# Threshold sums moved among ScalarE's waits, and the work between two attention groups reordered, in a fused four-layer graph network kernel

## The reference

```python
Xf = Xa = X = h
Z = 0
for n in range(2):
    q = Xa @ W1.T @ W2.T
    k = Xa @ W3.T
    probs = softmax(q @ k.T)                      # 2048 x 2048
    # keep the largest probabilities of a row until their sum reaches 0.9
    A = probs * mask;  A = A / A.sum(-1)
    Xf = rownormed(adj + I) @ Xf
    Xa = A @ Xa
    Z = Z + Xf @ U1[n].T + Xa @ U2[n].T
x = x + layernorm(X + Z) * ln_g + ln_b
```

## Time and profile before

| | |
|---|---|
| median of three executions | 1072.57 us (1072.10 to 1072.85) |
| the profiled execution's own time | 1073.61 us |
| its span, first to last instruction | 1071.8 us |
| TensorE busy (products) | 838.4 us, 78% |
| VectorE busy | 779.4 us, 73% |
| ScalarE busy | 509.2 us, 48% |
| GpSimd busy | 70.5 us, 7% |
| TensorE's mean granted clock | 0.894 of full speed |

### The profile page before, as it was taken

The page is one execution under the profiler, slowest core; times in us unless marked ns, Lnnn a source line. Parts: engine busy times, 40 slices in busy tenths (PEclk is TensorE's granted clock), DMA queues, the critical chain, the costliest instruction groups (busy, mean ns, idle before and its releaser), DMA issues.

```text
span 1071.8 us, 12286 instructions
## 1 busy us (share of the span) xinstructions
PE 838.4 (78%) x3886; PEld 563.7 (53%) x3886; DVE 779.4 (73%) x2363; ACT 509.2 (48%) x979; POOL 70.5 (7%) x68
## 2 busy tenths in 40 slices
PE   4879958887887843839778978868289899996795
PEld 4844325555655633737356557547258475553342
DVE  5978679888998998961797889789799502326715
ACT  4877235357367376314452664764765332023212
POOL 0020110000000000000000000010000200002201
PEclk9999987888988985969799789979689999998798
DMA  9949203334004000000044220220152546500001
GB/s 335 354 173 430 104 29 129 130 106 158 1 1 158 1 1 1 1 2 1 1 157 149 87 79 1 94 119 1 49 209 78 230 161 245 226 1 0 1 0 39
DMA packets 20221, 108.25 MB, mean 101 GB/s; under 512 B 1824, under 2 KB 8752, under 8 KB 9776
## 3 DMA queue, kind: packets, MB, share of 16 engines
q1 hardware_dynamic: 18752, 106.77, 26.7%
q10 hardware_dynamic: 1392, 0.61, 0.2%
HBM read 88.23 MB, written 19.14 MB: 100 GB/s over the span
## 4 chain that ended last, share of the span: by engine, by line
PE 47%; DVE 29%; ACT 11%; issue 9%; POOL 2%; DMA 1%; DVEq 1%; POOLq 0%; SPq 0%; ACTq 0%
DVE AT L1525 9%; PE PS L808 9%; PE PS L743 7%; PE PS L676 5%; PE PS L880 5%; PE PS L546 4%; DVE mxv L1664 4%; DVE nd L1528 3%; PE PS L1063 3%; PE PS L1039 3%; DVE AT L2111 2%; PE PS L1069 2%; ACT BC L1252 2%; ACT AT L1252 2%; ACT AT L1085 1%
## 5 line engine op out<-in xcount | busy, mean ns | idle before, releaser
L1085 ACT ACTIVATE AT<-PS 128x512 f32<-128x512 f32 (+2 forms) x240 | 118.2, 562 | 127.1 <-PE PS L546 107.8
L743 PE MATMUL PS<-K,ST 128*128 128x512 f32 x224 | 129.4, 731 | 15.7 <-ACT EA L1220 8.1
L546 PE MATMUL PS<-ident,AT 128*128 128x128 f32 x544 | 84.1, 289 | 42.5 <-DVE AT L1525 18.0
L1525 DVE SCALAR_TENSOR_TENSOR AT<-EA,se 128x2048 uint8<-128x2048 f32 (+1 forms) x46 | 107.6, 2345 | 1.6 <-DVE se L1518 0.3
L1525 DVE SCALAR_TENSOR_TENSOR AT<-AT 128x2048 uint8<-128x2048 f32 (+2 forms) x48 | 96.1, 2002 | 1.8 <-PE PS L546 0.8
L1664 DVE TENSOR_REDUCE mxv<-PS 128x1 f32<-128x2048 f32 x32 | 73.3, 2289 | 30.4 <-PE PS L743 24.7
L546 PEld LDWEIGHTS PS<-ident,AT 128*128 128x128 f32 x544 | 67.5, 150 | 50.9 <-DVE AT L1525 18.9
L743 PEld LDWEIGHTS PS<-K,ST 128*128 128x128 f32 x224 | 50.6, 238 | 78.1 <-issue 78.0
L2111 DVE MAX8 AT<-AT 128x8 f32<-128x256 f32 x256 | 87.6, 411 | 0.7
L808 PE MATMUL PS<-hr,AT 128*128 128x128 f32 x512 | 69.2, 284 | 8.5 <-ACT AT L1085 7.7
L808 PE MATMUL PS<-AT 128*128 128x128 f32 x512 | 67.4, 279 | 10.2 <-ACT AT L1085 9.7
(11 more groups left out here) (297 smaller groups left out, 1471.1 us busy)
## 6 DMA issues: line engine op xcount, KB each, us to landing
AT<-keep_at SPq DMA_DIRECT2D x32, 1024.0 KB, 5.1
EA<-in_adj SPq DMA_DIRECT2D x20, 1024.0 KB, 6.8
keep_at<-AT SPq DMA_DIRECT2D x8, 2048.0 KB, 24.9
AT<-keep_at SPq DMA_DIRECT2D x8, 2048.0 KB, 12.2
AT<-in_adj SPq DMA_DIRECT2D x12, 1024.0 KB, 5.7
EA<-keep_degrees SPq DMA_DIRECT2D x1, 1024.0 KB, 6.4
keep_x<-K SPq DMA_DIRECT2D x4, 256.0 KB, 8.6
out<-EA SPq DMA_DIRECT2D x4, 256.0 KB, 2.3
```

Source lines behind the costliest of these rows:

```text
L546: return pe.transpose(dst, src, ident[0:p, 0:p])
L743: mm = pe.matmul(bank(half(gi, k) + n), ST[1][:, k * P:(k + 1) * P], wide_keys[:, n * BK:(n + 1) * BK], start=True, stop=True)
L1085: return act.activation(dst, src, ACT.Copy)
L1525: return dve.scalar_tensor_tensor(out=o, in0=x0, scalar=s, in1=x1, op0=op0, op1=op1, **k)
```

## The change

It moves instructions and adds no computation; no operand and no transfer is changed.

1. **TensorE, first round of a step.** A unit's product can be cut in halves. The logits of tile 2 go ahead of the rows of unit 1, and those of tile 3 between the halves of unit 2.
2. **ScalarE, first round.** The first-threshold sums of tiles 0 and 1 (four passes) no longer stand behind the queries: the first goes between the copy and the rows of the fourth unit, the second ahead of the queries, the third between the two query copies, the fourth behind them.
3. **ScalarE, second and third round** (the third only in step 0): one pass behind the last attended tile's fourth copy, one ahead of the queries (where there are any).
4. **ScalarE, every attended group's last tile:** `guess` goes ahead of the copy of the previous tile's result, where it stood behind it.
5. **VectorE, the six groups that have a successor in their step:** the last tile's mass goes ahead of the checks of `doubtful`, and these interleave with the sums.
6. **Step 1, third and fourth round:** the second norm and scaling of block 0 move ahead of the first-threshold sums; the norm of block 1 moves from the start of the fourth round to the third; its turning and summing on TensorE move one tile up.

```diff
 # TensorE
-            def unit_sums(u):
+            def unit_freed(u):
+
                 if u == UNITS:
                     pe.wait_ge(un_row, UNITS)
                 if u > 0:
                     pe.wait_ge(un_st, u)
                     pe.wait_ge(un_row, min(u, UNITS))
+
+            def unit_part(u, h):
+
+                p, c = u // UNITS, u % UNITS
                 left = hr if p == 0 else Xf
-                for j in range(NT):
-                    if j % HALF == 0:
-                        pe.wait_ge(slab_in[j // HALF], 16 * (u + 1))
+                pe.wait_ge(slab_in[h], 16 * (u + 1))
+                for j in range(h * HALF, (h + 1) * HALF):
...
-            def unit(step, g, u, early=False):
+            def unit_begun(step, g, u, early=False):
...
-                unit_sums(u)
+                unit_freed(u)
+                unit_part(u, 0)
+
+            def unit(step, g, u, early=False):
+
+                unit_begun(step, g, u, early)
+                unit_part(u, 1)
                 unit_rows(u)
...
-                if normed is not None and k - normed in (1, 2):
-                    rows_turned(normed, k - normed - 1)
+                if normed is not None and k in (1, 2):
+                    rows_turned(normed, k - 1)
...
-                    if normed == 1:
-                        pe.wait_ge(exT_ok, G * gi + k + 1)
-                        rows_summed(normed, 1)
...
+                            at = units_by(NB * step) + k
                             if k > 0:
                                 logits(step, 1, k)
-                            if k < UNITS_IN[NB * step]:
-                                unit(step, 0, units_by(NB * step) + k, True)
+                            if k == 2:
+                                unit_rows(at - 1)
+                            if k == 3:
+                                unit_part(at - 1, 1)
+                                unit_rows(at - 1)
+                            if k == 1 or k == 2:
+                                unit_begun(step, 0, at, True)
+                            if k == 1:
+                                unit_part(at, 1)
+                            if k == 0 or k == 3:
+                                unit(step, 0, at, True)
...
 # ScalarE
-            def queries(step, g):
+            def queries(step, g, between=None):
...
                 copy(ST[0][0:DA, :], bank(7)[0:DA, :]).then_inc(t1_out, 1)
+                if between:
+                    between()
                 act.wait_ge(q_mm, gi + 1)
...
+            def one_below(step, g, m, k, f):
+
...
+                act.activation(act_junk[f], E[:, k, :], ACT.Relu if f == 0 else ACT.Sign, scale=-1.0,
+                               bias=th[:, k:k + 1], accum_out=below[:, f, k:k + 1]).then_inc(sum_ok, 1)
...
                     copy(stg[b % 2], bank(4 + b % 2)).then_inc(e_copied, 1)
+                    if b == 1 and between:
+                        between()
                     if b == 1 and k > 0:
                         result_out(k - 1)
-                    if b == 1 and between:
-                        between()
                     if b == 2 and inside:
                         inside()
+                if copied:
+                    copied()
...
-                    if normed == 0:
-                        first_scaled(0)
-                    elif normed == 1:
-                        first_norm(1)
+                    if normed is not None:
+                        first_scaled(normed)
                     for k in range(G):
                         if g > 0:
-                            attend(step, g - 1, k, (lambda: guess(step, g + 1)) if more and k == G - 1 else None, normed,
-                                   inside=(lambda: exponential(step, g + 1, 1)) if more and k == 0 else None)
-                            if normed == 1 and k == 0:
-                                first_scaled(1)
+                            ends = more and k == G - 1
+                            attend(step, g - 1, k, (lambda: guess(step, g + 1)) if ends else None, normed,
+                                   inside=(lambda: exponential(step, g + 1, 1)) if more and k == 0 else None,
+                                   copied=(lambda: one_below(step, g + 1, 0, 0, 0)) if ends and normed is None else None)
+                            if ends and normed is None:
+                                one_below(step, g + 1, 0, 0, 1)
...
-                        if g == 0:
-                            if k == G - 1:
-                                guess(step, 1)
+                        if g == 0 and k != 2:
                             unit_next()
+                        if g == 0 and k == G - 1:
+                            guess(step, 1)
+                            unit_sums(u)
+                            one_below(step, 1, 0, 0, 0)
+                            unit_rows(u)
+                            u += 1
+                            one_below(step, 1, 0, 0, 1)
                     if g < NB - 2:
-                        queries(step, g + 2)
+                        queries(step, g + 2, (lambda: one_below(step, 1, 0, 1, 0)) if g == 0 else None)
+                    if g == 0:
+                        one_below(step, 1, 0, 1, 1)
                     if more:
-                        sums_below(step, g + 1, 0, (0, 1, 2))
-                        unit_next()
-                        if step == 1 and g == 1:
-                            first_norm(0)
                         if normed == 0:
                             second_norm(0)
-                            sums_below(step, g + 1, 1, (0,))
+                            sums_below(step, g + 1, 0, (0,))
                             second_scaled(0)
-                        sums_below(step, g + 1, 1, (1,) if normed == 0 else (0, 1))
+                            sums_below(step, g + 1, 0, (1, 2))
+                        else:
+                            sums_below(step, g + 1, 0, (2,) if g == 0 else (1, 2))
+                        unit_next()
+                        if step == 1 and g > 0:
+                            first_norm(g - 1)
+                        sums_below(step, g + 1, 1, (0, 1))
                         unit_next()
                         sums_below(step, g + 1, 1, (2,))
...
 # VectorE
+            def doubtful_with_sums(nq, n):
+
+                mass_above(EA if n % 2 == 0 else EB, n, G - 1)
+                v.wait(1)
+                v.put(tt(s_(3), s_(3), s_(4), ALU.max))
...
+                dve.wait_ge(sum_ok, sums_by(n, 0) + 2 * (G - 1))
+                v.put(stt(pa, below[:, 1, :], float(N), ALU.add, nq.th, ALU.mult))
...
+                crossing_checked(q)
                 if left > 1:
                     logit_mean(gi + 2)
-                crossing_checked(q)
-                doubtful()
-                if left > 0:
-                    last_tile(nq, gi + 1)
-                    surplus_below(nq, gi + 1, 0)
-                    last_surplus(nq)
+                if left == 0:
+                    doubtful()
+                else:
+                    doubtful_with_sums(nq, gi + 1)
```

59 lines of the change are left out of this document (37 added, 22 removed).

## The result

| | before | after |
|---|---|---|
| median | 1072.71 us (1072.10 to 1073.60, 4 runs) | 1086.65 us (1086.12 to 1087.79, 4 runs) |
| ratio, 95% interval | | 1.0131 (1.0113 to 1.0148) |
| span of the profiled execution | 1071.8 us | 1086.0 us (the slowest of its four) |

The account below looks back on a forecast made before the run. No engine bounds it throughout; a chain changing engines does, without slack from ScalarE's second query copy. Terms 3.0 + 2.6 + 0 + 0.8 + 2.5 - 6.2 = +2.7 us gave 1075.3 us against the median, range 1067.5 to 1080.0.

Parts of the forecast that it names:

- (d): Guess ahead of the result's copy: TensorE's projection starts 1.1 us later, offset by a 1.1 gain in step 0's third round.
- First rounds, TensorE's order: First rounds' earlier logits: VectorE 4.6 us earlier at its cut, fourth unit ready at 225.7, nothing gained.
- First rounds, passes: ScalarE's passes among its first-round waits: second query copy +2.6 us; total +3.0 in step 0, +0.8 in step 1.
- (e): Second rounds, ScalarE's pass behind the last attended tile's fourth copy: +0.6 us.
- (f): Second rounds, ScalarE's pass ahead of the queries: +0.8 us with the issue.
- Checks: VectorE's interleaved checks in step 0's third round: gain 1.1 us, for a round total of 0.
- Tail: Step 1 from the third round on, norms reordered: -6.2 us (-7.8 to -3.6), GpSimd's last root slipping ahead of VectorE's masks.
- boundary gives nothing away: Rival, chance 0.21: next logits don't hang on the second query copy, four boundary terms fall to 0; -6.5, 1066.1 us.
- passes hide better: Rival, chance 0.17: first query product at half clock in other rounds too, (b) and (f) cost nothing; 1072.3 us.
- the tail doesn't pay: Rival, chance 0.20: GpSimd's root starts behind VectorE's first mask, -3.6 to -4 instead of -6.2; 1077.7 us, up to 1080.
- five terms ahead of the tail: Step 0's first, second, third rounds +3.0, +2.6, 0; step 1's first and second +0.8, +2.5 us.

Follow-up runs that it names:

- e7: Kernel before with only ScalarE's four first-round passes moved among its waits: 1076.53 us, ratio 1.0046.
- e13: Changed kernel with VectorE's old checks restored and the mean of the logits ahead of the exact cut: 1087.59 us, ratio 1.0148 to the kernel before.
- e4: Kernel before with only VectorE's interleaved checks, the mean of the logits behind the exact cut: 1071.44 us, ratio 1.0001.
- e11: Kernel before with step 1's reordered norms and VectorE's interleaved checks, the mean behind the exact cut: 1070.83 us, ratio 0.9990.
- e14: Changed kernel without TensorE's new first-round order and the four first-round passes: 1084.97 us, ratio 1.0129 to the kernel before.
- e15: Same instructions as e11, kernel before with reordered norms and interleaved checks, run for a second profile: 1071.73 us, ratio 0.9992.
- e9: Kernel before with only ScalarE's early passes of the second rounds and step 0's third round: 1077.72 us, ratio 1.0040.
- e12: Kernel before with both first-round parts, TensorE's new order and ScalarE's four passes: 1080.64 us, ratio 1.0071.
- e3: Kernel before with only the reordered norms in step 1's third and fourth round: 1065.59 us, ratio 0.9935.
- e10: Same as e3, only the reordered norms in the kernel before, measured again: 1067.39 us, ratio 0.9946.
- e18: Same as e3, only the reordered norms in the kernel before, a third comparison: 1067.78 us, ratio 0.9954.
- e5: Changed kernel with TensorE's projection put behind the next blocks turned and multiplied: 1079.29 us, ratio 1.0055 to the kernel before.
- e2: Kernel before with only the guess moved ahead of the result's copy: 1081.60 us, ratio 1.0083.

## Why the prediction was wrong

1. **The step that failed: (d), guess ahead of the result's copy, "starts 1.1 us later".** The wait itself was right (1.07 us at 309.22). I took it as the whole price and, in step 0's third round, as paid by the checks' gain. The runs show 2.9 us in each of three rounds, 1.2 for the wait and 1.7 for the clock behind it. I had used the clock for the units and for the logits behind a longer wait, and not for a gap of one microsecond inside a dense stretch. Forecast for it 3.3 us in all, measured 9. In step 1's third round I had counted nothing, and nothing is what it costs; that was luck, for I hadn't seen that TensorE has other products at that place.
2. **First rounds, TensorE's order: "ready at 225.7 ... Nothing gained".** The VectorE side was right (4.9 us earlier at its cut, and wasted). That the fourth unit would not be later was wrong: +2.1 in the trace after, 3.0 us measured alone.
3. **First rounds, passes:** +2.5 for 2.6 at the second query copy in the trace after, but 4.1 in e7; alone 4.9 us in all where 3.8 was forecast.
4. **Later passes (e), (f):** +1.30 for 1.4 at the second query copy in the trace after. Over the whole kernel 4.3 to 5.8 for 2.8: the products behind that copy take 1.6 us longer as well, and I had given them no clock.
5. **The mean's place** was a part of the diff that the prediction left out. It costs nothing in the changed kernel (with the mean ahead, e13, the first round is 0.2 us longer) and 2.2 or 2.3 us in the profiles of the four kernels whose first round isn't late already (e4, e11, e14, e15). The costs measured alone (8.9, 7.6, 4.3, and -1.1 for tail and checks together) sum to 19.7 us where the change costs 14.0: the parts share waits and falls of the clock, so neither alone nor undone is the price.
6. **Checks:** 1.2 us saved where 1.1 was forecast, in the third round of step 0.
7. **Tail:** -4.6 in the trace after; alone -4.9 to -7.0 for -6.2, of which 4.8 to 5.3 lie in the stretch that was changed. The root was to be either short or stretched; it was in between (2.84 us), since each of its three instructions meets the masks by itself: the third began inside a mask and ended with it. By the rule that I had cited from the Trainium skill, page "SBUF — State Buffer", section "Who interferes with whom", that is what an instruction does that comes second, and I had wrongly applied it to the three as one. The trace doesn't bear the rule out whole: the second instruction, begun 0.16 us ahead of the mask, ran beside it for 0.85 us, and neither took longer than elsewhere; spans on GpSimd are rough in these profiles.

The rival "boundary gives nothing away" is ruled out by e7, e9 and e12, "passes hide better" by the same, "the tail doesn't pay" by e3, e10 and e18. The true case, four of the five terms ahead of the tail above my upper end (all but step 1's first round), was none of my rivals; its price stood in my rows as the 24 products in 13.49 and in 10.54 us.

## What to carry to other kernels

When an instruction is put ahead of a copy that TensorE waits for, price the stretch behind the wait too, by what the windows show of the granted clock behind the nearest waits of that size; if it must stand there, give TensorE other work at that place, which got 8 of 9 us back in e5, and which the summed rows did by themselves in step 1's third round. A wait that ScalarE has anyway is no free place for a pass either, if TensorE waits for what comes behind it. And ask of every line of a diff, also of one that only changes sides with its neighbour as the mean did, who waits for it in the slowest and in the fastest version of the round.

## What the runs showed of the hardware

- Behind a wait of 2.15 us on TensorE, which every version has, come 1.16 us of products at full clock. Where a new wait of 1.07 us followed these, the granted clock fell to 0.50 in 15 of 15 places, for 3.4 us in after and 6.8 in e2 at the place shown. Without the new wait it fell in 8 of 45 such places.
- The clock also falls where nothing was changed. Between 63 and 70 us it was down in the profile after and not in that of before, with the same instructions; the maximum at 172.85 us before lay between 1.1 us earlier and 2.7 later in the profiles of the eighteen experiments. In the three profiles of the tail alone, the stretch from 326.71 to 350.93 us before is 1.9 us shorter and the one ahead of it, from 291.98 on, 1.6 us longer, with the same instructions: the fall lies at another place, and the two nearly cancel. In the comparisons the kernel before took 1068.2 to 1075.3 us where it is counted. One profile therefore can't carry a difference of 2 us, unless the same place repeats in several.
